# Time mixing: column-tiled sums, row-tiled decays, and keys and receptances in plain fp32 inside the scan

## What is computed

```
xn = layernorm(x);  sx = token_shift(xn)
h  = tanh((xn + sx * maa_x) @ maa_w1)             # five groups of 32
xw, xk, xv, xr, xg = xn + sx * (maa_stack[i] + h[i] @ maa_w2[i])
w  = exp(-exp(time_decay + tanh(xw @ decay_w1) @ decay_w2))
r, k, v, g = xr @ Wr, xk @ Wk, xv @ Wv, silu(xg @ Wg)
# per head of 16 key and 16 value channels, over the tokens:
out[t] = r[t] @ (u * k[t]^T v[t] + S);  S = w[t] * S + k[t]^T v[t]
x2 = x + (groupnorm(out) * g) @ Wo
```

## Time and profile before

| | us |
|---|---|
| median of 3 runs | 3131.51 |
| lowest, highest | 3130.46, 3132.37 |
| the profiled execution's own time | 3133.62 |
| its span, first to last instruction | 3131.8 |

### The profile page before, as it was taken

One profiled execution on the slowest core, in us unless ns is written; L12 is line 12 of the kernel. 1 busy time (PEld: TensorE's weight loads), 2 busy tenths in 40 slices (PEclk: granted clock), 3 DMA queues, 4 the chain that ended last, 5 costly groups with the idle time before them and its releaser, 6 DMA issues.

```text
span 3131.8 us, 41273 instructions
## 1 busy us (share of the span) xinstructions
PE 2970.3 (95%) x14832; PEld 2313.4 (74%) x14832; DVE 1842.0 (59%) x2694; ACT 1195.6 (38%) x2584; POOL 527.7 (17%) x363
## 2 busy tenths in 40 slices
PE   6898999999696999999999999999999999999899
PEld 3445454454475888888888887878888888888787
DVE  6988979889575444446444446464444554444644
ACT  4233242332343443434443434344434344343432
POOL 2655636556000000001000001010000000000100
PEclk8999999999898999999999999999999999999999
DMA  4001010000224111111111111121111111111011
GB/s 130 21 11 41 7 45 7 19 29 0 96 80 161 65 45 45 31 53 37 54 37 54 37 50 54 40 78 54 37 54 37 54 38 33 51 36 44 27 50 58
DMA packets 54721, 148.84 MB, mean 48 GB/s; under 512 B 6128, under 2 KB 7664, under 8 KB 53520
## 3 DMA queue, kind: packets, MB, share of 16 engines
q1 hardware_dynamic: 51760, 143.88, 13.9%
q0 software_dynamic: 2880, 3.94, 0.7%
HBM read 131.28 MB, written 12.58 MB: 46 GB/s over the span
## 4 chain that ended last, share of the span: by engine, by line
PE 65%; DVE 2%; ACT 1%; issue 0%; DMA 0%; ACTq 0%; DVEq 0%
PE ca_ps L60 19%; PE ca_ps L62 19%; PE ca_ps L61 18%; PE ca_ps L1907 4%; PE ca_ps L1923 4%; PE ca_ps L1915 2%; PE ca_ps L1949 1%; DVE ca_stats L68 0%; DVE ca_xres L1684 0%; DVE ca_ctx_lo L1715 0%; DMA ca_xres<-in_ctxT 0%; DVE ca_wq_lo L1642 0%; ACT ca_sk L1600 0%; ACT L1600 0%; DVE ca_h_lo L1709 0%
## 5 line engine op out<-in xcount | busy, mean ns | idle before, releaser
L1684 DVE TENSOR_TENSOR ca_xres<-ca_xres,ca_ps 128x512 f32<-128x512 f32 x384 | 264.1, 688 | 243.4 <-PE ca_ps L62 238.4
L1471 ACT ACTIVATE ca_pr<-ca_ps,ca_nb 128x129 f32<-128x129 f32 x512 | 182.4, 369 | 511.2 <-DVE ca_nb L1667 511.0
L60 PE MATMUL ca_ps<-ca_h_hi,ca_wq_hi 128*128 128x512 f32 x768 | 312.7, 407 | 4.8 <-DVE ca_h_lo L1709 4.3
L606 DVE TENSOR_TENSOR_SCAN tm_xn<-tm_wd,tm_vb 128x512 f32<-128x512 f32 x256 | 298.5, 1208 | 8.6
L62 PE MATMUL ca_ps<-ca_h_hi,ca_wq_lo 128*128 128x512 f32 x768 | 302.4, 394 | 0.0
L61 PE MATMUL ca_ps<-ca_h_lo,ca_wq_hi 128*128 128x512 f32 x768 | 300.3, 391 | 0.0
L60 PE MATMUL ca_ps<-ca_wv_hi,ca_ctx_hi 128*128 128x256 f32 x1024 | 298.0, 291 | 0.0
L62 PE MATMUL ca_ps<-ca_wv_hi,ca_ctx_lo 128*128 128x256 f32 x1024 | 287.6, 281 | 0.0
L61 PE MATMUL ca_ps<-ca_wv_lo,ca_ctx_hi 128*128 128x256 f32 x1024 | 287.3, 281 | 0.0
L1424 POOL TENSOR_TENSOR ca_dv<-ca_bvr 128x256 f32<-128x256 f32 x32 | 23.7, 742 | 1453.7 <-DVE ca_v L1652 1443.7
L60 PE MATMUL ca_ps<-ca_wo_hi,ca_ct_hi 128*128 128x512 f32 x640 | 253.5, 396 | 0.2 <-DVE ca_xres L1684 0.2
(11 more groups left out here) (244 smaller groups left out, 6213.5 us busy)
## 6 DMA issues: line engine op xcount, KB each, us to landing
ca_sq<-in_wq SPq DMA_DIRECT2D x49, 512.0 KB, 5.5
ca_so<-in_wo SPq DMA_DIRECT2D x48, 512.0 KB, 3.6
ca_sk<-in_wk SPq DMA_DIRECT2D x33, 512.0 KB, 6.5
ca_sv<-in_wv SPq DMA_DIRECT2D x32, 512.0 KB, 3.7
ca_bvr<-in_bvb SPq DMA_DIRECT2D x32, 256.0 KB, 3.9
tm_xq<-in_x SPq DMA_DIRECT2D x16, 256.0 KB, 2.6
tm_xres<-in_x SPq DMA_DIRECT2D x4, 1024.0 KB, 5.2
x_dram<-tm_xres SPq DMA_DIRECT2D x4, 1024.0 KB, 4.6
```

Source lines behind the costliest of these rows:

```text
L60: pe.matmul(out, lhs[0], rhs[0], start=first, stop=False)
L606: v.tensor_tensor_scan(state[t % 2][:, d, :], wd[:, g].rearrange("p b t -> p (b t)"), pair[:, d, :], 0.0, ALU.mult, ALU.add).then_inc(scan ...
L1471: ins = act.activation(pr[hd][:, b, :], ps[:, BANK_SC + b // 2, o:o + KW], ACT.Exp, bias=nbs[hd][:, b:b + 1], scale=SCALE, accum_out=sms[h ...
L1684: v.tensor_tensor(xres[U.h][:, U.quad * 4 + b, :], xres[U.h][:, U.quad * 4 + b, :], ps[:, BANK_O + b % 2, :], ALU.add).then_inc(o_out, 1)
```

## The change

**Sums.** PE's `accumulate` runs at every second step for two steps at once: four fp32 products of 32 columns each, one for each group of 32 columns of the array. State columns, `pick_k`, `spread_v` and `s0` are renumbered to fit. **Decays.** The 64 hidden rows are computed twice (`dec1` has 128 columns), and `decays(f)` issues two products, one on the upper 64 rows of the array and one on the lower, into two banks: after stage 0 and after stage 2. **Projections.** Keys and receptances are plain fp32 products of unsplit inputs `xk`, `xr` and weights `wk`, `wr`, group by group inside the scan, as the gates were. The key stage, the splits of these inputs (ACT, POOL) and weights (ACT, DVE, q = 0) and their waits are gone; key block 0 stands before the scan, receptance block 0 behind the first two spreads. **Value split.** `value_lo` of block 0 stays before the scan; blocks 1 to 3 follow DVE's steps 4, 12 and 20. `value_hi` of these stands at ACT's steps 0 to 2.

The core of the diff (renamings and loads left out):

```
             def accumulate(q, t):
-                g = t // 8
-                if t % 8 == 0 and g >= 2:
+                g, u = t // 8, t % 8 // 2
+                if u == 0 and g >= 2:
                     pe.wait_ge(cent_out, q * 8 + (2 * g - 2))
-                pe.wait_ge(rs_ready, q * STEPS + (t + 1))
-                for e in range(2):
-                    d = 2 * (t % 8) + e
-                    at = 71 - (64 * (d // 8) + d % 8)
-                    ins = pe.matmul(mx[g % 2][:], pick_k[:, at:at + P], prod[t % 4][:, e, :], start=d == 0, stop=d == 15)
-                ins.then_inc(rs_used, 1)
+                pe.wait_ge(rs_ready, q * STEPS + (t + 2))
+                for k in range(4):
+                    ins = pe.matmul(mx[g % 2][32 * k:32 * k + 32, :], pick_k[:, 3 - u:35 - u], prod[(t + k // 2) % 4][:, k % 2, :],
+                                    start=u == 0, stop=u == 3)
+                    if k % 2 == 1:
+                        ins.then_inc(rs_used, 1)
...
+                def decays(f):
+                    if f == 0:
+                        pe.wait_ge(lora_out, q * 3 + 3)
+                    else:
+                        pe.wait_ge(decay_out, q * 8 + 3)
+                    for k in range(2):
+                        pe.matmul(pj[(1 + k) % 2][:], dec2[64 * k:64 * k + 64, (f + k) * P:(f + k + 1) * P], h5[64 * k:64 * k + 64, :],
+                                  start=True, stop=True).then_inc(decay_full, 1)
...
+                def project(w, x, f, half, full):
+                    for c in (2 * half, 2 * half + 1):
+                        ins = pe.matmul(pj[1][:], w[:, c, f * P:(f + 1) * P], x[:, c, :], start=c == 0, stop=c == EC - 1)
+                    if half == 1:
+                        ins.then_inc(full, 1)
+
+                def key(f, half):
+                    if half == 0:
+                        if f > 0:
+                            pe.wait_ge(r_free, q * 4 + (f + 1))
+                        else:
+                            pe.wait_ge(decay_out, q * 8 + 8)
+                            pe.wait_ge(xf_ready, q * 24 + 16)
+                            if first:
+                                pe.wait_ge(wkr_in, 32)
+                    project(wk, xk, f, half, k_full)
...
-                stage(2, 0)
+                stage(0)
+                decays(0)
                 mix(q, 3, 2)
                 mix(q, 3, 3)
                 for c in range(1, EC):
-                    decay(c - 1)
-                    stage(2, c)
+                    stage(c)
+                    if c == 2:
+                        decays(2)
                     mix(q, 4, c - 1)
                     mix(q, 5, c - 1)
-                decay(3)
-                stage(3, 0)
+                key(0, 0)
                 mix(q, 4, 3)
+                key(0, 1)
                 mix(q, 5, 3)
-                for c in range(1, EC):
-                    stage(3, c)
+                if first:
+                    pe.wait_ge(w_hi_ready, 4)
+                spread(0)
+                spread(1)
                 receptance(0, 0)
-                if first:
-                    pe.wait_ge(w_hi_ready, 5)
-                spread(0)
                 receptance(0, 1)
-                spread(1)
                 for t in range(STEPS):
                     spread(t + 2)
-                    if t >= 1:
-                        accumulate(q, t - 1)
+                    if t >= 2 and t % 2 == 0:
+                        accumulate(q, t - 2)
                     for f in range(EC):
                         if t == 8 * f:
                             bonus(f)
-                        if f > 0 and t in (8 * f - 7, 8 * f - 5):
-                            receptance(f, (t - 8 * f + 7) // 2)
-                        if f < 3 and t in (8 * f + 5, 8 * f + 7):
-                            gate(f, (t - 8 * f - 5) // 2)
-                        if f == 3 and t in (25, 27):
-                            gate(f, (t - 25) // 2)
+                        if f > 0 and t in (8 * f - 7, 8 * f - 6):
+                            receptance(f, t - (8 * f - 7))
+                        if f > 0 and t in (8 * f - 5, 8 * f - 4):
+                            key(f, t - (8 * f - 5))
+                        if f < 3 and t in (8 * f + 5, 8 * f + 6):
+                            gate(f, t - (8 * f + 5))
+                        if f == 3 and t in (25, 26):
+                            gate(f, t - 25)
...
             def body(q, first):
                 for c in range(EC):
-                    mix(q, 4, c)
+                    mix(q, 4, c, first)
                     mix(q, 5, c, first)
-                if first:
-                    split_w(2)
-                for c in range(EC):
-                    value_lo(q, c)
+                value_lo(q, 0)
...
                         if t == 8 * f + 15 and f < 2:
                             gated(q, f)
+                        if t == 8 * f + 4:
+                            value_lo(q, f + 1)
```

More of the change, by code:

```diff
@@ L325, in normalised, with hi @@
                                scale=vec[:, VEC["ln1_w"] + c:VEC["ln1_w"] + c + 1]).then_inc(xn_ready, 1)
[L327 to L335, removed]
+            def hi(q, c, first):
+                act.wait_ge(xf_ready, q * (4 * J) + (4 + place(2, c) + 1))
+                if not first:
+                    act.wait_ge(f_full, q * 4)
                 act.activation(x_hi[:, c, :], xf[:, c, :], ACT.Copy).then_inc(hi_ready, 1)
@@ L393, in decay, with evacuate @@
                     act.activation(wd[:, f, :, 1:L], quad3(ew[:])[:, :, 0:L - 1], ACT.Exp, scale=-1.0).then_inc(decay_out, 1)
-                def evacuate(j, f):
-                    act.wait_ge(f_full, q * 8 + ((j - 2) * 4 + f + 1))
-                    if j == 3 and f == 0:
-                        for s in range(3):
-                            act.wait_ge(pack_in[s], (q + 1) * (48, 48, 144)[s])
-                    tile = vv if j == 2 else kk
-                    act.activation(tile[:, f, :, 1:L + 1], quad3(vb[:, f, :]), ACT.Copy).then_inc(f_free, 1)
+                def evacuate(f):
+                    act.wait_ge(f_full, q * 4 + (f + 1))
+                    if first and f == 0:
+                        act.wait_ge(pad_ready, 1)
+                    act.activation(vv[:, f, :, 1:L + 1], quad3(vb[:, f, :]), ACT.Copy).then_inc(f_free, 1)
                 def receptance(f):
@@ L407, in receptance, with key @@
                     act.activation(rr[:, f, :], pj[1][:], ACT.Copy).then_inc(r_free, 1)
+                def key(f):
+                    act.wait_ge(k_full, q * 4 + (f + 1))
+                    if f == 0:
+                        for s in range(3):
+                            act.wait_ge(pack_in[s], (q + 1) * (48, 48, 144)[s])
+                    act.activation(kk[:, f, :, 1:L + 1], quad3(pj[1][:]), ACT.Copy).then_inc(k_free, 1)
                 def value_hi(c):
-                    act.wait_ge(f_free, q * 8 + (c + 1))
+                    act.wait_ge(f_free, q * 4 + (c + 1))
                     for tile, p in v_halves:
@@ L481, in _ @@
                 normalised(0, c)
[L482 removed]
+            split_w()
             front(0, True)
```

211 lines of the change are left out of this document (91 added, 120 removed).

## The result

The changed kernel takes 3161.94 us (median of 4 runs, 3159.67 to 3163.83), the kernel before 3131.38 us beside it: ratio 1.0095, 95% interval 1.0082 to 1.0108. It is slower by 0.95%, some 30 us. The forecast was slower, 3140 us, with a range from 3103 to 3162. The side was right and the two losses inside the scans were named, but the loss is three and a half times the forecast's 8.8 us. That the range holds it, by 0.06 us, is luck: the forecast's own branch (A) ended at 3156. The profiled execution has a span of 3162.0 us (3131.8 before) and a mean granted clock of 0.961 (0.984).

What follows compares the result with a forecast made beforehand. DVE sets the scan's pace, PE close behind: -45.1 - 4.4 - 0.5 + 40.8 = -9.2 us, +18.0 for PE's clock = +8.8 on 3133.6, 3142.4; about 3140 us as median, range 3103 to 3162.

Steps and rivals of the forecast that it cites:

- branch (A): The forecast case for the whole kernel, slow clock included: about 3140 us, own range 3128 to 3156, chance 0.48.
- The subtractions: Six value subtractions a quarter moved into the scan, the second of each pair held by POOL: 3.4 us a pair, 40.8 lost.
- the two bounds below it (1.42 and 2.36): A subtraction pair in the scan: 1.42 us if nothing collides, 2.36 if the collision costs what the earlier trace's row says.
- rival C: Moved subtractions in the scan miss POOL's product or cost only the bare row: 1.42 to 2.36 us a pair; chance 0.12.
- Before the scan: Shorter waits for mixing products and fewer splits ahead of the scans: 11.8, 10.6, 12.1 and 10.6 us won, 45.1 in all.
- rival D: The tiled sums in the scan take turns: 12 us of stall a quarter, no clock loss, 3171 us; chance 0.06.
- The clock: PE idles in the scan behind steps 7, 15, 23 and before the first spread; its clock falls: 4.5 us a quarter, 18.0.
- rival B: PE's clock holds in the scan or its falls miss the bonus products: 0 for 18.0 us, 3122 us; chance 0.27.
- What DVE sees of it: In-scan stalls behind bonus products: 2.2 us shrink to about 0.7, 0.4 new at step 2; 4.4 us won in all.
- 5.8 in q = 2: DVE's waits for PE's mixing products before the scan of q = 2: 2.6 us against 8.4, 5.8 won.
- The joint is DVE and latency of unchanged parts: nothing: The joint between one quarter's scan and the next quarter's work: no gain or loss.
- what I don't see: Chance of 0.07 left for the unseen, such as a slow joint because PE idles over the last steps.

Runs made afterwards that it cites:

- experiment 2: Changed kernel with the two value subtractions behind steps 4, 12 and 20 parted, one behind that step and one behind the next: 3134.30 us, ratio 1.0003.
- experiments 1 to 4, 6 and 7: Changed kernel with: bonus copy later 3135.28; subtractions parted 3134.30; PE kept busy 3143.37; load later 3154.99; untiled sums 3216.79; copy, parting and load together 3107.17 us.
- experiment 3: Changed kernel with PE's spreads behind steps 7, 15 and 23 written 5, 7 and 7 times over: 3143.37 us, ratio 1.0034.
- experiment 5: Changed kernel with all value splits before the scan again, on ACT and DVE: 3124.32 us, ratio 0.9975.
- experiment 4: Changed kernel with the 1 MB load of the residual's input issued behind step 8 of the scan (last quarter's unmoved): 3154.99 us, ratio 1.0064.
- Experiment 10: Kernel of experiment 9 with spreads of steps 30 and 31 written 5 times, unpacks of step 30 three times: 3089.15 us, ratio 0.9865.
- experiment 9: Changed kernel with all value splits before the scan, bonus copy behind the next state write, and 1 MB load behind step 8: 3098.65 us, ratio 0.9895.
- experiment 8: Kernel before the change with one edit, ACT's copy of the bonus product at step 8f + 2 for 8f + 1: 3121.16 us, ratio 0.9970.

## Why the prediction was right, and where its size was off

**Right, by its own steps.** The subtractions: 3.4 us a pair, 40.8 in all; measured 3.6 and 43.3. The order of arrival in the earlier trace rows and POOL's full length were the right reading, and the two bounds below it (1.42 and 2.36) are what they cost elsewhere: parted they cost 1.55 (experiment 2), so rival C was a fact about another order. Before the scan: q = 0 and 1 to within 0.1 us, and term by term in q = 1 (waits for mixing products 2.4 for 2.6 us). So close a hit is luck in part: in the profiled executions of experiments 1 to 4, 6 and 7 the first scan starts at 75.3 to 78.1 us, and the stretch between the first two scans lasts 63.9 to 66.0 us. The tiles run together (rival D falls). The clock: it falls at the ends of the groups, and experiment 3 shows that the stalls at steps 10, 18 and 26 come from that; rival B, that it holds, falls. Their price was near: the forecast had 17.8 us of waiting at these steps in the four quarters (15.0 of its 18.0 for the clock, and 2.8 that it left to the full clock), and 18.7 were measured. By step it was less good: 1.6, 9.2 and 7.8 us were measured at steps 10, 18 and 26 of the four quarters, for 3.0, 6.0 and 6.0 forecast for the clock; and the full clock leaves no stall there.

**Too small, step by step** (21.4 us in all):

- "What DVE sees of it": at step 2 the prediction had 0.4 us new and half a fall of the clock (0.75 us), 4.6 us in four quarters. It was 8.2. In q = 2 PE idles before the first spread, and both spreads and most of the first receptance, up to 481.6 us, run at 0.50:

```profile
475.94 1.22 PE L772 MATMUL tm_vb<-tm_v_low_d,tm_spread_v 128*128 128x512 f32 x2 [3.06 <-DVE tm_v_high_d L554]
476.96 1.05 PE L772 MATMUL tm_vb<-tm_v_high_d,tm_spread_v 128*128 128x512 f32 x2
477.82 5.57 PE L777 MATMUL tm_pj<-tm_xr,tm_wr 128*128 128x512 f32 x8
```

  Behind them stand the receptance's copy, POOL's product, the bonus product, its copy and the state write of step 2. With the splits back (experiment 5) the wait goes, at the same slow clock, under cover. The scans' 8.8 us are these 3.6, 2.5 for the subtractions, 0.9 at steps 10, 18 and 26, 0.8 at step 29 and 1.0 in steps that are a little longer.
- "5.8 in q = 2", part of the 12.1 won before that scan: only 4.3 of the 12.1 came. Of the missing 7.8 us, 6.2 are the way back to the loop's start meeting the 1 MB load: experiment 4 gives them back. The prediction had no step for it. In the earlier trace rows the same place showed 3.81 us at 449.34 for 2.04 in q = 1. I counted this as won and did not ask why it is 1.8 us longer in the loop's second round. The trace of the kernel before answers it: PE's stage ahead of that product ran at a granted clock of 0.55 from 444.30 to 448.00, and at 1.00 at the same place of q = 1. DVE's way back lay under this wait for PE, with the same load issued at 444.75; what it cost there can't be seen. When PE became faster at this place, it came to light.
- "The joint is DVE and latency of unchanged parts: nothing": 2.5 us lost before q = 3, and most of the 1.6 us of q = 2's 7.8 that experiment 4 leaves there. DVE waits 1.78 and 0.78 us for the last sums at these two joints and does not wait for them before the change; at the joint before q = 1 it doesn't in this execution, but does for 1.3 us in that of experiment 3. PE idles over steps 28 to 31 as it does at 7, 15 and 23, and what was said of the one place was not carried to the other; it stood under what I don't see, with 0.07. Experiment 10 shows it, on the version of experiment 9.
- 2.5 us lie in unchanged code and are no step of the prediction.

The parts that were wrong by more than 2 us between or at the start of the scans all have one sign: each is a wait that opens when PE, made lighter, goes idle, or when a cover leaves. The forecast priced the ends of the groups well and the two ends of the scan badly.

## What to carry to other kernels

Price a moved instruction at the place where it lands, by who arrives just ahead of it: two subtractions cost 1.55 us apart and 3.60 us together. When a change makes lighter a PE that was busy nearly all the time, list every stretch in which it then idles and what stands right behind each, then shorten the queue behind it (here one copy a step later, 27 us) rather than the PE work. And before work is moved out of a stretch, name what it covers.

## What the runs showed of the hardware that was not expected

- DVE, on its way back to the start of its loop, waited 2.45 to 2.46 us with nothing to release it (experiments 4 and 9), and 5.75 us with a 1 MB load on the DMA engines at that moment. That the load makes the wait longer is shown by its removal. That it is a wait for instructions is read from the instruction packets in that stretch; how the load holds them up is not shown.
- A POOL instruction that arrives 0.11 us behind a DVE subtraction is recorded 0.44 us longer (2.80 for 2.36), so both engines lose.
- PE work that computes nothing new gained 19 us (experiment 3) and some 6 us (experiment 10); the granted clock was 1.00 there for 0.50 to 0.60 without it.

Open is what the projections' move into the scan is worth by itself: it was not undone alone. The best version, 3089 us, is 1.35% faster than the kernel before and about 1% faster than experiment 8; parts of the repairs (the load later) were not tried on the kernel before.
